# Q and K of one batch in four regions that change places from batch to batch

## The reference, cut to what matters

```python
q, k, v = split(x @ qkv_w.T)                    # 16 heads of 16 numbers
q, k = rotary(q), rotary(k)
heads 0..5:    softmax(q k^T / 4 + causal) v    # "dot" heads
heads 6..9:    tq, tk = sqrt(1/curv + |q|^2), sqrt(1/curv + |k|^2)
               arg = max(-curv * (q k^T - tq tk^T), 1 + 1e-7)
               softmax(1 / (1e-6 + sqrt(1/curv) * arccosh(arg)) + causal) v   # "hyperbolic" heads
heads 10..15:  softmax(4 * qn kn^T + causal) v  # q and k divided by their norms
x = layernorm(x + concat(heads) @ proj_w.T + proj_b)
h = gelu(ragged_dot(x.reshape(-1, 256)[tok], w1)); y = ragged_dot(h, w2)   # 8 experts, top 2
out = layernorm(x + scatter_add(y * weight) + bias)
```

## Time and profile before

| what | us |
|---|---|
| three runs | 1944.33, 1945.61, 1964.9 |
| median | 1945.61 |
| the profiled execution, its own time | 1951.51 |
| its span, first to last instruction | 1949.9 |
| TensorE busy | 1614.1 (83%) |
| ScalarE busy | 1392.6 (71%) |
| VectorE busy | 1201.2 (62%) |
| GpSimd busy | 755.3 (39%) |

### The profile page before, as it was taken

One profiled execution on the slowest core, in us unless ns is written; L12 is line 12 of the kernel. 1 busy time (PEld: TensorE's weight loads), 2 busy tenths in 40 slices (PEclk: granted clock), 3 DMA queues, 4 the chain that ended last, 5 costly groups with the idle time before them and its releaser, 6 DMA issues.

```text
span 1949.9 us, 38980 instructions
## 1 busy us (share of the span) xinstructions
PE 1614.1 (83%) x13082; PEld 908.0 (47%) x13082; DVE 1201.2 (62%) x3014; ACT 1392.6 (71%) x1460; POOL 755.3 (39%) x369
## 2 busy tenths in 40 slices
PE   7999958876986897799779977986898699779993
PEld 4655623333443443344344433443444344369992
DVE  6877846635865686477557765765685577532234
ACT  2655648896887888788878887887889788851220
POOL 3344244434343544353335435343534365530003
PEclk9999959988997998799889989998998899889997
DMA  4699850363044305500650155054306510368893
GB/s 156 214 240 275 229 165 12 88 93 73 9 70 95 78 2 88 138 18 2 110 122 13 27 98 119 2 76 99 69 2 110 124 35 30 121 210 277 285 331 102
DMA packets 75633, 214.94 MB, mean 110 GB/s; under 512 B 18048, under 2 KB 27520, under 8 KB 69600
## 3 DMA queue, kind: packets, MB, share of 16 engines
q1 hardware_dynamic: 66256, 179.10, 37.2%
q0 software_dynamic: 9200, 33.43, 5.6%
HBM read 143.88 MB, written 68.58 MB: 109 GB/s over the span
## 4 chain that ended last, share of the span: by engine, by line
PE 31%; issue 14%; DVE 9%; ACT 9%; POOL 7%; DMA 6%; SPq 3%; DVEq 0%; POOLq 0%; ACTq 0%
PE a_o L1222 5%; PE a_w L1267 4%; POOL a_Z L1495 4%; PE a_s L737 4%; PE a_s L725 4%; PE a_s L1207 4%; SPq L1125 3%; DVE xm L1739 3%; POOL a_R L1492 3%; DMA K<-t_parts 2%; PE a_w L1235 2%; PE a_w L1311 2%; ACT a_Z L1422 2%; DMA x_mid<-xm 2%; ACT a_PT L1404 2%
## 5 line engine op out<-in xcount | busy, mean ns | idle before, releaser
L1404 ACT ACTIVATE a_PT<-a_s 128x1024 f32<-128x1024 f32 (+3 forms) x576 | 459.6, 809 | 152.8 <-PE a_s L1210 88.7
L1495 POOL TENSOR_TENSOR a_Z<-a_Z,a_R 128x2182 f32<-128x2182 f32 x64 | 290.2, 4535 | 450.2 <-ACT a_R L1416 443.3
L1207 PE MATMUL a_s<-Q,K 96*128 96x512 bf16 (+7 forms) x1152 | 330.6, 352 | 97.8 <-ACT a_PT L1404 75.2
L1492 POOL TENSOR_TENSOR a_R<-a_Z 128x2182 f32<-128x2182 f32 x64 | 245.0, 3828 | 241.7 <-DVE a_Z L1607 205.9
L1615 DVE TENSOR_REDUCE a_mx<-a_w 128x1 f32<-128x512 f32 (+2 forms) x576 | 307.2, 550 | 44.2 <-PE a_w L1235 37.9
L1607 DVE TENSOR_SCALAR_CACHE_REDUCE a_Z<-a_w 128x512 f32<-128x512 f32 (+7 forms) x384 | 202.8, 528 | 123.0 <-PE a_w L1250 74.3
L1222 PE MATMUL a_o<-a_PT,a_V 128*32 128x512 f32 (+3 forms) x1536 | 183.9, 555 | 78.6 <-ACT a_PT L1404 47.7
L1267 PE MATMUL a_w<-ident,a_R 128*128 128x128 f32 (+1 forms) x1152 | 207.2, 307 | 39.5 <-DVE a_PTh L1661 19.7
L1661 DVE COPY a_PTh<-a_w 128x512 f32<-128x512 f32 (+1 forms) x256 | 158.4, 622 | 107.0 <-PE a_w L1267 105.1
L1235 PE MATMUL a_w<-K,Q 96*128 96x512 bf16 (+2 forms) x576 | 188.9, 334 | 26.1 <-DVE a_mx L1615 10.5
L1207 PEld LDWEIGHTS a_s<-Q,K 99*128 99x128 bf16 (+1 forms) x1152 | 111.4, 103 | 193.9 <-ACT a_PT L1404 109.8
(11 more groups left out here) (170 smaller groups left out, 2613.0 us busy)
## 6 DMA issues: line engine op xcount, KB each, us to landing
qk_parts<-pm SPq DMA_DIRECT2D x128, 192.0 KB, 3.4
Q<-in_w SPq DMA_DIRECT2D x46, 512.0 KB, 6.2
K<-in_w SPq DMA_DIRECT2D x46, 512.0 KB, 7.2
Q<-qk_parts SPq DMA_DIRECT2D x144, 128.0 KB, 5.2
K<-qk_parts SPq DMA_DIRECT2D x144, 128.0 KB, 8.0
v_rows<-p_vt SPq DMA_DIRECT2D x8, 2048.0 KB, 10.3
a_V<-v_rows SPq DMA_DIRECT2D x24, 512.0 KB, 7.8
xm<-in_xt SPq DMA_DIRECT2D x8, 1024.0 KB, 8.8
```

The lines of the kernel that those rows point to most:

```text
L1207: m = pe.matmul(sB[x % 2][:, i, 0:w], Kb[0:r, h, P * j:P * j + P], Qb[0:r, h, t0:t0 + w], start=True, stop=not diag)
L1404: act.activation(PT[:, u % 2, 2 * k:2 * k + 2, 0:w], sB[x % 2][:, :, 0:w], ACT.Exp, scale=scale_of(GROUPS[g][2 * k])).then_inc(prob.sem, 1)
L1492: pool.tensor_tensor(r, z, z, ALU.mult).then_inc(z_sq.sem, 1)
L1495: pool.tensor_tensor(z, z, r, ALU.add).then_inc(z_sum.sem, 1)
```

## The change

1. `region(b, g)` says in which of four regions of four slots group g of batch b lies. Batch 0 has group g in region g. For the next batch group 3 gets the region of group 0, group 0 that of group 1, group 1 that of group 3, and group 2 stays. `slot_of(b, h)` gives a head's slot, and the matmuls on Q and K use it.
2. SP loads for the next batch: group 3 after step 11, group 0 after step 23, group 1 after the last argument, group 2 after step 35 as before. Each group is now one run, so group 1 takes 12 transfers of 128 KB. The three rows of ones that the dot heads 4 and 5 need in K are loaded with it, one transfer of 12 KB from a new input.
3. SP and TensorE are written out for all turns, without a loop. DVE and POOL have turn 1 before their loops.
4. `x_mid` is written for batch 0 only (`is_routed`). For other batches `add_bias` waits for the normalization that stands before it on DVE.
5. The first round of row maxima stands in steps 3 to 8 (six steps) in place of 2 to 8 (seven). The list of the tail gives whatever is left to its last tile.
6. The expert weights of a tile lie in one run of 2048 columns, so a tile takes two transfers of 1 MB in place of four of 512 KB.

```diff
+def region(b, g):
+    at = {0: 0, 1: 1, 2: 2, 3: 3}
+    for _ in range(b):
+        at = {3: at[0], 0: at[1], 1: at[3], 2: at[2]}
+    return at[g]
+
+def slot_of(b, h):
+    g = next(g for g, heads in enumerate(GROUPS) if h in heads)
+    return 4 * region(b, g) + BLOCKS[BLOCK_OF[g]].index(h)
+
+def head_loads(g, b, qk_parts, t_parts, ones, Qb, Kb):
+    found, block, s0 = [], BLOCK_OF[g], 4 * region(b, g)
+    if g == 1:
+        found.append((g, Kb, KR, KR + 3, (slot_of(b, N_DOT - 2), slot_of(b, N_DOT - 1) + 1, ones)))
...
-HEAD_RUNS = {0: ((12, 16),), 1: ((4, 6), (10, 12)), 3: ((HYP0, COS0),), 2: ((0, 4),)}
...
-    HOME = (6144, 7168), (2048, 5120), (3072, 4096), (0, 1024)
+    HOME = [region(B - 1, g) * 2 * FF for g in (0, 1, 3, 2)]
...
-        ROUNDS = (((4, 5), 1, 2, 7), ((0, 1, 2, 3), 2, 9, 12))
+        ROUNDS = (((4, 5), 1, 3, 6), ((0, 1, 2, 3), 2, 9, 12))
...
                 sp.wait_ge(valued.sem, valued.before(b, 11))
-                heads(0)
+                heads(3)
                 if not first:
                     values(0)
-                hold(sp, valued.sem, valued.before(b, 23), sp_passed)
+                sp.wait_ge(valued.sem, valued.before(b, 23))
+                heads(0)
+                values(1)
+
+                sp.wait_ge(wide_full.sem, wide_full.before(b, wide[last_argument]))
                 heads(1)
-                values(1)
-
-                hold(sp, wide_full.sem, wide_full.before(b, wide[last_argument]), sp_passed)
-                heads(3)
-
-                hold(sp, valued.sem, valued.before(b, NQ - 1), sp_passed)
+
+                sp.wait_ge(valued.sem, valued.before(b, NQ - 1))
                 heads(2)
                 values(2)
...
-            with nc.Fori(1, B, engines=[sp.engine], hint_back_edge=True) as b:
+            for b in range(1, B):
                 turn(b)
...
-            with nc.Fori(1, B, engines=[pe.engine], hint_back_edge=True) as b:
+            for b in range(1, B):
                 turn(b)
...
                 elif kind == "mid_out":
-                    rows_out(d, x_mid, 0, mid_sent)
+                    if is_routed(d):
+                        rows_out(d, x_mid, 0, mid_sent)
...
                 elif kind == "add_bias":
-                    dve.wait_ge(mid_sent.sem, mid_sent.at(d))
+                    if is_routed(d):
+                        dve.wait_ge(mid_sent.sem, mid_sent.at(d))
+                    else:
+                        dve.wait_ge(normed.sem, normed.at(d, 0))
```

More of the change, by code:

```diff
@@ L558, in _ @@
             pool.wait_ge(padded, 2)
-            pool.memset(ahead["K"][KR:KR + 3, 0:N_DOT, :], 1.0).then_inc(ahead["ones"], 1)
+            pool.memset(ahead["K"][KR:KR + 3, slot_of(0, 0):slot_of(0, 3) + 1, :], 1.0).then_inc(ahead["ones"], 1)
             pool.wait_ge(ahead["ones"], 1)
@@ L602, in _ @@
             low(B - 1, 3)
-def head_loads(g, runs, b, qk_parts, t_parts, Qb, Kb):
-    found, block = [], BLOCK_OF[g]
+def region(b, g):
[10 more added lines that the diff above has]
+        found.append((g, Kb, KR, KR + 3, (slot_of(b, N_DOT - 2), slot_of(b, N_DOT - 1) + 1, ones)))
     for qk, buf, order in ((0, Qb, QPART), (1, Kb, KPART)):
         for r, part in enumerate(order):
[L611 to L615, removed]
+            src = qk_parts[b:b + 1, qk, part, 2 * BR * block:2 * BR * (block + 1), :]
+            found.append((g, buf, r * HD, (r + 1) * HD, (s0, s0 + 4, src.rearrange("o (d h) t -> d (o h) t", d=HD))))
     if g == 3:
@@ L673, in load @@
         e = sp.value_load(self.route["own"][0:1, t:t + 1], min_val=0, max_val=NE - 1)
[L674 to L678, removed]
+        for m, w in enumerate((self.w1, self.w2)):
+            sp.dma_start(w[:, self.HOME[i]:self.HOME[i] + 2 * FF],
+                         self.io["w12"][bass.ds(e, 1), :, 2 * m * FF:2 * (m + 1) * FF]
+                         .rearrange("o p f -> (o p) f")).then_inc(self.w_here[i], 16)
     def load_rows(self, sp, k):
@@ L997, in attend, with is_routed @@
                 "rows_out", "shift")
+        def is_routed(d):
+            return isinstance(d, int) and d == 0
         def is_late(item):
@@ L1022, in attend @@
                 finish += [("second", t - 1), ("y_copy", t - 1)]
-            take = SIZES[t] if t < len(SIZES) else 0
+            take = SIZES[t] if t < len(SIZES) - 1 else len(waiting)
             finish, waiting = finish + waiting[:take], waiting[take:]
@@ L1123, in heads @@
                     if not first:
-                        for _, buf, lo, hi, (a, z, src) in head_loads(g, HEAD_RUNS[g], b, qk_parts, t_parts, Qb, Kb):
+                        for _, buf, lo, hi, (a, z, src) in head_loads(g, b, qk_parts, t_parts, io["ones"].bitcast(BF16).rearrange("r (h t) -> r h t", h=2), Qb, Kb):
                             sp.dma_start(buf[lo:hi, a:z, :], src).then_inc(qk_here[g].sem, 16)
@@ L1564, in _ @@
             pool.wait_ge(others, 16 * NOTHER)
-            with nc.Fori(1, B - 1, engines=[pool.engine], hint_back_edge=True) as b:
+            turn(1)
+            with nc.Fori(2, B - 1, engines=[pool.engine], hint_back_edge=True) as b:
                 turn(b)
@@ L1780, in _ @@
             dve.wait_ge(others, 16 * NOTHER)
-            with nc.Fori(1, B, engines=[dve.engine], hint_back_edge=True) as b:
+            turn(1)
+            with nc.Fori(2, B, engines=[dve.engine], hint_back_edge=True) as b:
                 turn(b)
@@ L1828, in shape_constants @@
         "ident": np.eye(P, dtype=np.float32),
+        "ones": np.full((3, T), 0x3F803F80, dtype=np.uint32).view(np.float32),
         "tabs": tabs,
@@ L1888, in build @@
             Kb = inner.enter_context(nc.sbuf_tensor("K", [P, H, T], BF16))
-            loads = {g: head_loads(g, runs, 0, qk_parts, t_parts, Qb, Kb) for g, runs in HEAD_RUNS.items()}
+            loads = {g: head_loads(g, 0, qk_parts, t_parts, io["ones"].bitcast(BF16).rearrange("r (h t) -> r h t", h=2), Qb, Kb) for g in (0, 1, 3, 2)}
             xm = inner.enter_context(nc.sbuf_tensor("xm", [P, 2, CK * T], F32))
@@ L1904, in build @@
                      "parts_sent": [Event(ctx, nc, f"parts_sent{k}", 4, 16) for k in range(4)],
-                     "Q": Qb, "K": Kb, "loads": [load for g in HEAD_RUNS for load in loads[g]],
+                     "Q": Qb, "K": Kb, "loads": [load for g in loads for load in loads[g]],
                      "ones": ctx.enter_context(nc.semaphore("ones")),
-                     "qk_here": {g: Event(ctx, nc, f"qk_here{g}", 1, 16 * len(loads[g])) for g in HEAD_RUNS}}
+                     "qk_here": {g: Event(ctx, nc, f"qk_here{g}", 1, 16 * len(loads[g])) for g in loads}}
             project(nc, io, qk_parts, t_parts, v_rows, route, ahead)
```

21 lines of the change are left out of this document (10 added, 11 removed).

## The result

| | median of the runs, us | ratio to before, 95% interval |
|---|---|---|
| before | 1943.88 (20 runs) | |
| changed | 1936.74 (20 runs) | 0.9946 [0.9927, 0.9965] |

The change gives 0.5%, some 10 us, where 34.7 us were forecast. The time lies above the range (1892 to 1930). By the bound of 1% it is no change, for which the chance was 0.17. The profiled execution has a span of 1935.7 us.

A forecast was written before the change was run, and what follows sets the result against it. It took a batch in `attend` as a ring of waits, the expert tiles as TensorE-bound; 10.8 + 25.5 + 1.6 − 3.2 = 34.7 us off the profiled 1951.5 gives 1916.8, against the median 1910.9 us; range 1892 to 1930.

The forecast's parts named there:

- Step 2: No `x_mid` write after batch 0, so DVE's waits go: 3.4 us a batch for six batches, bounds 1.5 and 3.7.
- Step 1: Group 3 loaded 50 us ahead, TensorE's wait goes: 10.8 us at batch 0's end, 0.85 at six other ends.
- Step 3: First round of row maxima in six steps: costs 0.4 us a batch, times 8, so −3.2 us.
- Steps 4 and 5: Group 1 loaded late, ones one more transfer, at batch ends; TensorE and SP written out: each counted 0.
- Step 6: Tail: TensorE's wait after the last `x_mid` write goes, 1.6 us (bounds 0 and 2); 1 MB weight transfers 0.
- The first: Rival: at batch ends the `out` write with POOL's load and addition keeps the period; gain 16.6 us, 1929.0 us; chance 17%.
- the `out` path: Batch end: write of `out`, 10.86 us, into POOL's addition; forecast as nearly as long as the path through group 3.
- The second rival: Batch ends: `out` lands sooner, ACT's wait goes, all DVE waits count; gain 58.6 us, 1887 us; chance 13%.
- Group 1 landing late: Rival: TensorE stops at a batch's first maximum for group 1, 7.7 us a batch; about 1965 us; chance 4%.

The follow-up runs named there:

- e6: Kernel before with only the `x_mid` write limited to batch 0 (turn 1 ahead of the loops); ratio to before 1.0006.
- e2: Changed kernel with `x_mid` written for all eight batches again; ratio to the kernel before 0.9927.
- e10: Changed kernel with `x_mid` written for all batches and the first round of maxima in seven steps again; ratio to the kernel before 0.9926.
- e1: Changed kernel with the small 1e-5 addition taken off DVE (POOL adds it); ratio to the kernel before 0.9826, median 1907.58 us.
- e5: Changed kernel with the 1e-5 addition off DVE and POOL's load of x placed behind the last unit's addition; ratio to the kernel before 0.9734.
- e11: Changed kernel with the 1e-5 addition off DVE, load of x later, first maxima in seven steps; ratio to the kernel before 0.9720, median 1890.71 us.
- e3: Changed kernel with `x_mid` written for all batches and the 1e-5 addition off DVE; ratio to the kernel before 0.9893.
- e9: Changed kernel with the 1e-5 addition kept on DVE but in the accumulating form; ratio to the kernel before 0.9819.
- e12: Changed kernel with only POOL's load of x moved behind the last unit's addition; ratio to the kernel before 0.9898.

## Why the prediction was wrong

**Step 2 is the step that failed.** It stood with 3.4 us a batch, 20.4 us for six. It measured nothing: e6 gives 1.0006, and e2 against the changed kernel has the other sign, 0.0019. The working added up waits behind DVE's wait: TensorE's 3.6 us for DVE and ACT's 2.12. It took them for waits for the `x_mid` write. Their last cause was another. Behind DVE's wait, which ended at 1149.91, POOL's addition ran from 1153.21 to 1158.01, and DVE's small instruction of 1157.02 could not end before it. Had it come 3.37 us sooner, at 1153.65, it would have stood beside the same addition. ACT's next logarithm needs that addition too. The hint stood in the trace of before: L1733 with 1.03 us, where an equal instruction takes 0.17. L1739 was another hint: its 128 executions take 0.60 us on average, the shortest 0.39. I read the waits in brackets and not the durations. The bound below, 1.5 us, was wrong for the same reason; it should have been 0.

**Step 1** was right at the end of batch 0, where 10.8 us were forecast. From ACT's L1419 on the last unit of batch 0 to the one on the first unit of batch 1 it was 34.5 us (445.78 to 480.32); in the changed kernel it is 22.9 (447.65 to 470.50), 11.7 less, and in e10 23.5, 11.0 less. The 5.1 us for the other six ends no run can tell: e10 measured 0.0074, 14 us, with an interval of 5 us to either side, and the 11.0 us with the tail's 2.8 make that up. ACT still waits for POOL's addition at these ends, 1.4 to 2.1 us in batches 1 to 6 of the changed kernel.

**Step 3** was right in sign and about in size: −3.2 forecast, 0 to −3 measured. **Steps 4 and 5**: no wait for group 1 or the ones, TensorE and SP written out within the noise of e10.

**Step 6**, the tail, has no run of its own. From ACT's L1419 on the last unit of batch 7 (1729.40, in the changed kernel L1433 at 1718.02) to the end of the span it was 220.5 us and is 217.7, 2.8 less where 1.6 were forecast. But the reason was not the write of `x_mid`: e10 and e2, which write it for every batch, have 217.7 and 217.6 us, and TensorE's wait of 1.60 us is gone in them too. Step 2 alone (e6) has 219.9. Which of the other parts gives it, the larger transfers or the new places, stays open.

Without step 2 the sum is 14.3 us; the measured ratio gives 10.5, with an interval of 3.7 us to either side.

**The rivals.** The first had 1929 us because the write of `out` takes over. Its neighbourhood was right (the gain of DVE is spent), its mechanism came second: e1 shows the lock in front of it (23 us), e5 the `out` path behind (18 us). Its sum still held 6 x 1.5 us for step 2. The second rival, with both paths shrinking, needs what e5 does by hand: e5 and e11 lie at 1892 and 1891 us, near its 1887, but by two more edits. Group 1 landing late did not happen.

**The marks I had set.** "The prediction as a whole is wrong if POOL's wait for `out` grows by what DVE gained": it did not, and the prediction was wrong all the same. There were seven such waits before, not six: one of 7.5 us is booked under "issue" in that profile. They took 44.8 us in all, 6.4 a time, and take 40.0 now, 5.7 a time. The mark that did tell is the distance from batch to batch, 181.5 us where about 178 were to come; it does not say why. None of my marks named an engine that is busy longer with the same instructions.

**What stays open.** In the changed profile the granted clock was at its lower level for some 20 us in batch 0, around the end of the first round of maxima. ACT lost 4.9 us there against the kernel before, over the first two units of the batch. A window of 22 us in the changed kernel (columns as in the earlier trace rows, the clock third from the end):

```profile
304.00:326.00 22.00, 19.59 (x99) 8.12 (x99) 11.17 (x30) 14.00 (x15) 5.38 (x2) 0.53 0.01 2
```

The same window in e3:

```profile
304.00:326.00 22.00, 16.77 (x127) 7.56 (x127) 13.89 (x40) 17.14 (x18) 5.62 (x3) 0.92 0.01 2
```

A matmul of four 128x128 blocks took 1.06 to 1.12 us there and 0.66 at the upper level. Both kernels have the maxima in six steps. The long low stretch is in the profiles of the changed kernel, e1 and e2, not in e3, e5, e9 and e12, and in none of the profiles with seven steps. So step 3 may cost through the clock in some executions; one profile for each kernel does not settle it.

No run touches the other lock, the normalization L1739 or L1755 beside POOL's square. It holds DVE some 3.5 us a batch in seven batches of the kernels before, changed and e11 alike. Whether anything waits for that is not shown.

## What to carry to other kernels

Ahead of every term "this wait goes, so all behind it gains", look at what else ends at the same time, in durations too: an instruction several times longer than its equals is waiting inside its record. Here a 128x8 addition from SBUF to SBUF on VectorE stood beside a GpSimd instruction of 4.8 us and was held to its end; the accumulating form cost a line and gave 1.3%, the move to other engines 1.2%. Where one wait after another is taken away, measure them together: step 2 gave 0 alone, nothing clear of noise with the held instruction gone in the old layout, and 13 us with both that instruction and the late load gone.

## What was not expected of the hardware

- The plain 128x8 instruction on DVE took 0.17 us alone and up to 4.58 us beside a two-input GpSimd instruction, ending 0.03 us after it. The plain 128x256 normalization took 0.41 us, and up to 3.92 beside GpSimd's square. The accumulating form took 0.16 us beside the same instruction (e9).
- The copies from PSUM (0.69 us) and the statistics from SBUF (0.42 us) ran beside it unchanged.
- The granted clock stayed near the lower level over the same 22 us in three profiles (0.53, 0.64 and 0.58), and was 0.92 there in e3, which is the changed kernel with two edits later in the batch.
